# Weight preparation of the FFN taken apart into 256 small units and woven into the attention phase (Trainium2, 8 cores)

## What is computed

```python
q = X @ Wq.T + bq; k = X @ Wk.T + bk; v = X @ Wv.T + bv     # X: (16, 2048, 1024)
scores = q @ k.T / 32, masked with -inf where j > i
attn = softmax(scores, axis=-2)                             # over the i axis
x = layernorm(X + attn @ v)
act_quant(x)    = clip(round(x * 127 / max|x|), -128, 127) / that scale    # per row
weight_quant(w) = clip(round(w / mean|w|), -1, 1) * mean|w|                # one mean per matrix
h = silu(depthwise_conv1d(act_quant(x) @ weight_quant(w1).T))              # w1: (4096, 1024)
x = layernorm(x + act_quant(h) @ weight_quant(w2).T)                       # w2: (1024, 4096)
```

## Time and profile before

| | us |
|---|---|
| device time, median of 2 runs (3911.14 to 3950.22) | 3930.68 |
| the profiled execution | 3908.41 |
| its span, slowest core (others 3884.7 to 3905.3) | 3906.8 |
| its busy time: PE, DVE, ACT, POOL | 2041.8, 1415.5, 1179.6, 197.3 |

### The profile page before, as it was taken

The page is one execution under the profiler, slowest core; times in us unless marked ns, Lnnn a source line. Parts: engine busy times, 40 slices in busy tenths (PEclk is TensorE's granted clock), DMA queues, the critical chain, the costliest instruction groups (busy, mean ns, idle before and its releaser), DMA issues.

```text
span 3906.8 us, 39637 instructions; the slowest of 8 cores (3884.7 to 3906.8 us)
## 1 busy us (share of the span) xinstructions
PE 2041.8 (52%) x10824; PEld 1129.2 (29%) x10824; DVE 1415.5 (36%) x4009; ACT 1179.6 (30%) x3058; POOL 197.3 (5%) x304
## 2 busy tenths in 40 slices
PE   0008962441498334200000577877777777778775
PEld 0003420110143111100000444544444444445442
DVE  0102043321102433205140445555555544455554
ACT  0001322220033222220300544444444444444442
POOL 2100001001000011002010000000000000000000
PEclk9999985665699666655555788888788888888887
DMA  1653002224300222242554100000000000000000
GB/s 34 196 145 57 1 11 78 62 65 131 63 1 1 54 70 62 63 129 77 191 161 86 50 24 19 25 28 17 28 28 28 28 28 28 25 20 23 28 12 22
DMA packets 197021, 214.63 MB, mean 55 GB/s; under 512 B 142850, under 2 KB 159426, under 8 KB 194756
## 3 DMA queue, kind: packets, MB, share of 16 engines
q1 hardware_dynamic: 175620, 138.61, 13.4%
q0 software_dynamic: 21184, 73.50, 5.5%
HBM read 105.02 MB, written 73.48 MB: 46 GB/s over the span
## 4 chain that ended last, share of the span: by engine, by line
PE 38%; DMA 22%; DVE 19%; issue 10%; ACT 9%; POOL 1%; DVEq 1%; ACTq 0%; POOLq 0%; SPq 0%
PE bank L920 10%; PE bank L801 8%; PE bank L461 6%; DMA PR_w<-w 5%; PE bank L553 4%; DVE F_u L908 4%; PE bank L822 3%; PE bank L442 3%; DVE Fg L911 3%; DMA s_xbf<-A_xbf 3%; DMA F_W2qT<-s_w2i 3%; PE bank L497 2%; DMA s_w1i<-PR_obf 2%; DMA A_xT<-s_xbf 2%; ACT F_D L814 2%
## 5 line engine op out<-in xcount | busy, mean ns | idle before, releaser
L801 PE MATMUL bank<-F_xq,F_W1qT 128*128 128x258 bf16 x4096 | 649.2, 311 | 0.0
L920 PE MATMUL bank<-F_W2qT,Fg 128*128 128x512 bf16 x2048 | 525.6, 395 | 45.1 <-ACT F_ev L932 38.9
L801 PEld LDWEIGHTS bank<-F_xq,F_W1qT 128*128 128x128 bf16 x4096 | 452.0, 111 | 179.1 <-issue 27.4
L827 ACT ACTIVATE Fg<-bank,cbc 128x256 bf16<-128x256 f32 x512 | 241.8, 472 | 736.8 <-PE bank L822 726.5
L822 PE MATMUL bank<-F_hs,F_D 128*128 128x256 bf16 x1536 | 286.7, 301 | 228.0 <-DVE F_hs L807 110.5
L807 DVE TENSOR_TENSOR F_hs<-bank,F_fbc 128x258 bf16<-128x258 f32 x512 | 216.9, 424 | 338.8 <-PE bank L822 302.3
L920 PEld LDWEIGHTS bank<-F_W2qT,Fg 128*128 128x128 bf16 x2048 | 203.2, 100 | 261.4 <-issue 92.6
L621 PE MATMUL xb<-iden_bf,PV_xqbf 128*128 128x128 bf16 x256 | 63.3, 265 | 405.9 <-DVE PV_xqbf L615 368.6
L822 PEld LDWEIGHTS bank<-F_hs,F_D 128*128 128x128 bf16 x1536 | 144.4, 104 | 314.5 <-issue 290.2
L814 ACT ACTIVATE F_D<-iden_f,w0c 128x128 bf16<-128x128 f32 x512 | 200.0, 391 | 64.2 <-DMA s_w2i<-PR_obf 64.2
L839 DVE TENSOR_TENSOR F_Mx<-F_Mx,Fg 128x256 bf16<-128x256 bf16 x496 | 143.3, 289 | 204.5 <-ACT Fg L827 196.8
(11 more groups left out here) (129 smaller groups left out, 2117.0 us busy)
## 6 DMA issues: line engine op xcount, KB each, us to landing
A_x<-x SPq DMA_DIRECT2D x32, 512.0 KB
PV_xsrc<-x SPq DMA_DIRECT2D x32, 512.0 KB
s_xln<-PV_xln POOLq DMA_DIRECT2D x32, 512.0 KB, 3.5
PR_w<-w SPq DMA_DIRECT2D x32, 512.0 KB
PR_w<-w SPq DMA_DIRECT2D x8, 2048.0 KB
F_xlnt<-s_xln SPq DMA_DIRECT2D x32, 512.0 KB
out<-F_xlnt POOLq DMA_DIRECT2D x32, 512.0 KB, 3.0
F_xq<-s_xqT SPq DMA_DIRECT2D x128, 64.5 KB
```

The source lines that it names most:

```text
L801: p.op("PE", lambda e, s=s, e8=e8, bk=bk, par=par: e.matmul(out=B[bk][:, 0:258], lhsT=F_W1qT[e8][:, s * 128:(s + 1) * 128], rhs=F_xq[par][ ...
L827: p.op("ACT", lambda e, s=s, par=par: e.activation(out=F_g[par][s][:], in_=B[2][:, 0:256], func=AF.Silu, bias=cbc[:, s:s + 1], scale=1.0), ...
L920: p.op("PE", lambda e, par=par, tb=tb, h=h, cs=cs, bk=bk: e.matmul(out=B[bk][:], lhsT=F_g[par][cs][:, tb * 128:(tb + 1) * 128], rhs=F_W2qT ...
```

## The change

`prep()` is gone. Its work is cut into units of 128x512 elements, 64 per matrix and pass, kept in a queue (`prep_q`). `drain(n)`, put at the end of each step of attention's loops, takes the next n units off the queue and writes their operations into the list there. There are two kinds:

- `_p1` (first pass): a DMA of 256 KB issued from **ACT**, and an ACT `Abs` with a running sum, in place, in one of two buffers.
- `_p2` (second pass): the same DMA again from ACT, the three DVE operations, and a POOL store of 128 KB.

The queue holds 64 `_p1` of w1, its mean, 64 `_p1` of w2, its mean, 64 `_p2` of w1, 64 `_p2` of w2: 258 entries. `drain` is called with 1 in the x load (16 steps), v (32) and q and k (64), with 2 in scores (16) and with 3 in PV (16): 192 places per sequence. So sequence 0 takes the first 192 entries and sequence 1 the last 66: 16 in its x load, 32 in its v stage, 18 in its q stage. The matrices are now read from DRAM twice. To make room, the attention probabilities `A_P` are packed (row block jt keeps only its T - 128 jt columns); the unit buffers lie behind. ACT's DMAs get a semaphore of their own ("AD").

```diff
-            stream = "PD" if (dma and eng == "POOL") else eng
+            stream = ("PD" if eng == "POOL" else
+                      "AD" if eng == "ACT" else eng) if dma else eng
...
-    A_P = [mem.at(OB + jt * 4096, f"A_P{jt}", [128, T], BF16) for jt in range(NT)]
+    A_P = [mem.at(OB + _ap_off[jt], f"A_P{jt}", [128, T - jt * 128], BF16)
+           for jt in range(NT)]
...
+    PR_in = [mem.at(PRS + i * 2048, f"PR_in{i}", [128, 512], F32)
+             for i in range(2)]
+    PR_ob = [mem.at(PRS + 4096 + i * 1024, f"PR_ob{i}", [128, 512], BF16)
+             for i in range(2)]
...
+            drain(1)     # end of an x-load step; also of a v group and of a q or k group
...
+            drain(2)     # end of a scores step
...
+            drain(3)     # end of a PV step
...
+    def _p1(m, u, wd, rows, cols):
+        col = 64 * m + u
+        up = (64 * m + u) % 2
+        p.op("ACT", lambda e, up=up, wd=wd, rows=rows, cols=cols: e.dma_start(
+            out=PR_in[up][:], in_=wd[rows, cols]),
+            writes=[f"pin{up}"], dma=True)
+        p.op("ACT", lambda e, up=up, col=col: e.activation(
+            out=PR_in[up][:], in_=PR_in[up][:], func=AF.Abs,
+            accum_out=PR_ap[:, col:col + 1]),
+            reads=[f"pin{up}"], writes=[f"pin{up}", f"pap{col}"])
...
+    def _p2(m, u, wd, sd, rows, cols, skey):
+        rwbk = f"rwb{m + 1}"
+        rwbc = RWB1 + m
+        up = (64 * m + u) % 2
+        p.op("ACT", lambda e, up=up, wd=wd, rows=rows, cols=cols: e.dma_start(
+            out=PR_in[up][:], in_=wd[rows, cols]),
+            writes=[f"pin{up}"], dma=True)
+        p.op("DVE", lambda e, up=up, rwbc=rwbc: e.tensor_scalar(
+            out=PR_in[up][:], in0=PR_in[up][:],
+            scalar1=misc[:, rwbc:rwbc + 1], scalar2=MAGIC,
+            op0=ALU.mult, op1=ALU.add),
+            reads=[f"pin{up}", rwbk], writes=[f"pin{up}"])
+        p.op("DVE", lambda e, up=up: e.tensor_scalar(
+            out=PR_in[up][:], in0=PR_in[up][:], scalar1=MAGIC, scalar2=1.0,
+            op0=ALU.subtract, op1=ALU.min),
+            reads=[f"pin{up}"], writes=[f"pin{up}"])
+        p.op("DVE", lambda e, up=up: e.tensor_scalar(
+            out=PR_ob[up][:], in0=PR_in[up][:], scalar1=-1.0, scalar2=None,
+            op0=ALU.max),
+            reads=[f"pin{up}"], writes=[f"pob{up}"])
+        p.op("POOL", lambda e, up=up, sd=sd, rows=rows, cols=cols: e.dma_start(
+            out=sd[rows, cols], in_=PR_ob[up][:]),
+            reads=[f"pob{up}"], writes=[skey], dma=True)
...
+    def drain(n=1):
+        for _ in range(n):
+            if prep_q:
+                prep_q.pop(0)()
...
+    build_prep_queue()
     for b in range(NB):
         attn(b)
-    if _cut != "attn":
-        if _cut != "noprep":
-            prep()
...
+    while prep_q:
+        drain(1)
+    ffn_entry()
```

More of the change, by code:

```diff
@@ L25 @@
 class Prog:
-    ENGINES = ("SP", "PE", "ACT", "DVE", "POOL", "PD")
+    ENGINES = ("SP", "PE", "ACT", "DVE", "POOL", "PD", "AD")
     def __init__(self):
@@ new lines, in _pmean @@
+    def _pmean(m):
+        base = 64 * m
+        p.op("DVE", lambda e, base=base: e.tensor_reduce(
+            out=misc[:, PMS:PMS + 1], in_=PR_ap[:, base:base + 64], axis=AX,
+            op=ALU.add),
+            reads=[f"pap{base + u}" for u in range(64)], writes=["pms"])
+        p.op("PE", lambda e: e.matmul(
+            out=B[5][0:1, 0:1], lhsT=misc[:, PMS:PMS + 1], rhs=onescol[:],
+            start=True, stop=True),
+            reads=["pms", "onescol"], writes=["B5"])
+        p.op("DVE", lambda e, m=m: e.tensor_scalar(
+            out=mw[:, 2 * m:2 * m + 1], in0=B[5][0:1, 0:1],
+            scalar1=1.0 / (H * E), scalar2=QCLIP, op0=ALU.mult, op1=ALU.max),
+            reads=["B5"], writes=[f"mw{m}"])
+        p.op("DVE", lambda e, m=m: e.reciprocal(
+            out=mw[:, 2 * m + 1:2 * m + 2], in_=mw[:, 2 * m:2 * m + 1]),
+            reads=[f"mw{m}"], writes=[f"rw{m}"])
+        p.op("PE", lambda e, m=m: e.matmul(
+            out=B[5][:, 0:2], lhsT=ones1[:], rhs=mw[:, 2 * m:2 * m + 2],
+            start=True, stop=True),
+            reads=[f"mw{m}", f"rw{m}", "ones1"], writes=["B5"])
+        p.op("DVE", lambda e, m=m: e.tensor_copy(
+            out=mwb[:, m:m + 1], in_=B[5][:, 0:1]),
+            reads=["B5"], writes=[f"mwb{m}"])
+        p.op("DVE", lambda e, m=m: e.tensor_copy(
+            out=misc[:, RWB1 + m:RWB1 + m + 1], in_=B[5][:, 1:2]),
+            reads=["B5"], writes=[f"rwb{m + 1}"])
@@ L1052, in build_program @@
     out_stores = []
-    import os as _os
-    _cut = _os.environ.get("KCUT", "full")
+    build_prep_queue()
     for b in range(NB):
         attn(b)
-    if _cut != "attn":
-        if _cut != "noprep":
-            prep()
-        if _cut not in ("prep", "noprep"):
-            ffn_entry()
-            ffn_loads(0)
-            ffn_loads_xlnt(0)
-            if _cut != "entry":
-                nch = NGC if _cut == "full" else min(NGC, int(_cut[1:]))
-                for gc in range(nch):
-                    ffn_chunk(gc)
-                if _cut == "full":
-                    ffn_tail()
+    while prep_q:
+        drain(1)
+    ffn_entry()
+    ffn_loads(0)
+    ffn_loads_xlnt(0)
+    for gc in range(NGC):
+        ffn_chunk(gc)
+    ffn_tail()
     p.op("POOL", lambda e: e.nop(), deps=out_stores)
```

115 lines of the change are left out of this document (34 added, 81 removed).

## The result

The changed kernel takes 4108.1 us, median of 11 runs (4093.2 to 4155.4); the kernel before took 3911.2 us in the same comparison (10 runs). The ratio is 1.049, 95% interval 1.046 to 1.052: slower by 5%. 4155 was forecast, 47 us too much, and the time lies in the range. But the sum hides errors of over 100 us in both directions: the terms that were too large are 158 us off together, those that were too small 106.

What follows compares the result with a forecast made beforehand. Prep was taken to stand alone on the critical path for 371.8 us with PE nearly idle. Nine costs sum to 617 us against 370 gained: net +247 on 3908.4, so 4155 us, range 4020 to 4310.

Steps and rivals of the forecast that it cites:

- v 1 and q 1 terms: v and q stages of sequence 1: second-pass units delay the evacuations, +47 us in v and +26 us in q.
- sign for term 2: v stage of sequence 0: if the 17th load goes out before this stage ends, the +120 us there falls away.
- term 2: v of sequence 0: 32 first-pass units wait for the last `A_WkT` load, then run ahead of ACT's first evacuation, +120 us.
- terms 2 and 3: Sequence 0: v, units ahead of the first evacuation, +120 us; q and k, 63 `_p1` between ACT's evacuations, +186 us.
- the issue overlaps the `Abs`: ACT's queue, rival: the next load may go out while the last `Abs` runs, 76 us less, 4079 us; chance 0.15.
- announced sign: q stage: evacuations 4.6 us apart after the first; under 3 us apart would mean hidden flights and a wrong forecast.
- term 5: PV of sequence 0: three loads behind each step's last copy delay DVE's residual additions, 6 us a step, +90 us.
- collisions: Rival: flights of 3.7 us beside POOL's stores and SP's loads, small stores stretched throughout, 4336 us; chance 0.1.
- term 6: x load of sequence 1: a 3.1 us unit store between any two of POOL's x stores, 16 times, +50 us.
- Scores: Scores of sequence 0: first-pass units overfill ACT's idle time and second-pass units delay DVE's mask and maximum, +74 us.
- the clock: First scores steps after the slow q and k stage: TensorE starts at a lower granted clock, +10 us (0 to 30).
- break-even: Whole change: gain and cost cancel at a load flight of 1.86 us; 2% faster only at 1.5 us.

Runs made afterwards that it cites:

- experiment 2: Changed kernel with 126 of the 128 first-pass loads left out, each `Abs` kept; 3927.7 us in a single run (before 3917.6).
- experiment 5: Changed kernel with each load issued two units ahead and a semaphore per buffer, so two are in flight; 3995.4 us in 4 runs, ratio to before 1.020.
- experiment 4: Changed kernel with the 32 units of sequence 0's v stage moved into its x load; 4062.1 us in a single run (before 3917.6).
- experiment 3: Changed kernel with one buffer for all units instead of two; 4253.7 us in a single run (before 3897.0).
- experiment 6: Changed kernel with the `s_xqT` store issued behind the three unit stores in sequence 0's PV steps; 4078.9 us in a single run (before 3897.0).
- experiment 7: Changed kernel with two loads in flight and the `s_xqT` store behind the three unit stores in PV; 3922.3 us in a single run (before 3918.4).
- Experiment 8: Changed kernel without units in sequence 1's x load, those 16 falling later; 4111.4 us in a single run (before 3918.4).
- Experiment 9: Against the kernel before: prep in 128x2048 tiles, first pass in sequence 0's x load (ACT loads), second beside q and k (SP loads); 3665.4 us, ratio 0.937.

## Why the prediction was right or wrong

**Right: the direction and its place.** Removing the prep stretch gave 369.9 us of 369.6. ACT waits out the flight of each load; the flight was 2.9 us against 3.0 taken; the units meant for the v stage could not start before the last `A_WkT` load had landed. Experiments 2 and 5 show the first, 4 the third. The v 1 and q 1 terms were right to 3 us, the first x load to 7. The sign for term 2 was badly worded: the 17th load went out at 384.32, 1.8 us before the end of the last v evacuation on that core (386.09), which by its letter refutes the term, and yet all 32 units stood ahead of the first q evacuation.

**Wrong: "a `_p1` holds ACT for 3.0 + 0.8 + 0.1 = 3.9 us" (terms 2 and 3).** It holds it for 3.0 us: 94.6 us from 384.3 to the first evacuation at 478.9, for 32 units, so that this came at 479 and not near 500. The next flight begins while the `Abs` still runs, and so the 0.8 us of the `Abs` cost nothing. The rival "the issue overlaps the `Abs`", to which I gave 0.15, was true. The "second buffer is of no use" was false: it is worth 0.4 to 0.8 us a unit (experiment 3). And in q and k I added 0.75 us for the evacuation on top, which also lies inside the flight; no rival had this. A group took 3.12 us (196.6 / 63), not 4.65. Together 306 us predicted and 178 measured. The announced sign stands on this: evacuations were 3.1 us apart on average, and 11 of the 63 distances on core 1 lay under the "under 3 us" that I had named as a refutation (2.76 the shortest), though flights were exposed and not hidden. That threshold was badly chosen.

**Wrong: term 5, "6 us a step", 90 against 146.** I laid three flights of 3.1 us end to end and let POOL's stores run beside them at no cost. The `s_xqT` store alone has a median flight of 5.6 us in the kernel before already, which I had not looked at. The steps became 29 us on core 1 and 27.5 on most others, and not 26. The second flight takes 7.2 us beside the `s_xqT` store in the step shown (6.2 in the median of that core, 4.6 to 5.2 on the six cores where the term was 121 to 125), and a chain of POOL stores and DVE's output buffer stands behind it. Experiments 5 to 7 show two chains of nearly the same length. My rival "collisions" named it but with flights of 3.7 us, for all alike.

**Wrong: term 6, 50 against 88.** The unit's store on POOL took 5.3 us and not 3.1, and lengthened the store of x by 0.5: (5.3 + 0.5) x 16 = 93. Experiment 8 gave back 72 to 78.

**Scores:** 74 and 10 for the clock forecast, 57 measured. Of this 12 to 17 hang on the first pass's loads (experiment 2). The clock's share is not separated by an experiment. The granted clock over the scores was 0.70 against 0.86 before, and the matmuls were busy for 79.4 us instead of 70.1, which bounds it at some 9 us.

The errors were -128 and -27 (scores) against +56 and +38. The total was nearer than its terms deserved: that they cancelled was luck. The break-even at a flight of 1.86 us rested on 3.9 us units too; experiment 2 shows that with all first-pass flights gone the kernel comes only to 3928, even with before, since PV and the x load keep their cost.

## What to carry to other kernels

Background work is free only if no engine that the foreground needs waits inside it: a load standing directly ahead of its user on an in-order engine turns that engine's idle time into the foreground's delay. So choose, stage by stage, the engine that has nothing to do, issue loads from a queue whose waits nobody stands behind, and use large tiles. Experiment 9 changed place, engine and tile size at once and does not say what each is worth; for the tile there is the flight alone, 5.2 us in the median for 1 MB against 2.9 for 256 KB. When a delay is taken away and the time moves too little, look for a second chain of the same length before giving the theory up (experiments 5, 6 and 7).

## What the runs showed of the hardware that was not expected

- ACT issued its next DMA 0.10 us after the start of a 0.63 us activation that stood ahead of it, since nothing made it wait for that activation's result. With one buffer, where something did, the issue came 0.80 us after the start (experiment 3).
- A load of 256 KB took 7.2 us beside a store of as many bytes in 256-byte pieces, 2.7 and 3.2 us for the two beside it in that step, and 2.9 in the median of all. A small store took 5.35 us behind loads of 1 MB, 3.8 beside loads of 512 KB, 2.2 alone.
- PV of sequence 0 has two lengths, though its code is the same, and neighbouring cores (0 and 1, 2 and 3, 4 and 5, 6 and 7) always stood at the same one: in the changed kernel 463 to 464 us on cores 0 and 1, 438 to 442 on the others; in experiment 4 475 to 479 on 0, 1, 4 and 5, 445 to 449 on the others; in experiments 2 and 8 474 to 482 on all but 4 and 5, 443 to 451 on these. The kernel before took 314 to 317 on every core. So the slowest cores of two single runs can differ by some 25 to 40 us from this alone. What the neighbours share that does it no run here shows.
- In experiment 9 the granted clock of core 4 in q and k was lower than on core 1, beside nearly the same rate of transfers, and the same 512 matmuls took longer: the stage took 131 us on cores 4 and 5 and 109 on the six others (columns as in the windows above, core 4 first; on core 1 the last 20 us of this window are already scores). Why is open.

```profile
464.00:596.00 132.00, 131.15 (x495) 54.81 (x504) 59.83 (x48) 42.99 (x63) 15.96 (x16) 0.81 0.52 183
```

```profile
464.00:596.00 132.00, 125.26 (x572) 55.97 (x569) 66.69 (x65) 47.20 (x72) 15.71 (x16) 0.98 0.53 185
```
